# A state-space layer and a mixture of experts: read-backs turned ahead of weight splits in the routed tiles, and the choice of experts in five parts

## The reference

```
attention half:  x = layer_norm(feat);  x = x @ in_proj.T (1024 -> 96);  conv of 3 taps, silu
                 selective scan over the rows (96 channels, 16 states);  out = y @ out_proj.T + feat
feed-forward:    scores = sigmoid(x @ router_w)                      # 32 experts in 8 groups of 4
                 4 groups by the sum of their two best scores; in them the 8 best experts of a row
                 weights = their scores, made to sum to 2.5
                 routed = sum over the 8 of weight * (silu(x @ gate_e) * (x @ up_e)) @ down_e
                 shared = silu(x @ sw_gate) * (x @ sw_up) @ sw_down
                 out = routed + shared + the attention half
```

## Time and profile before

| | |
|---|---|
| timed runs | 11768.19 us median of 3 (11751.63 to 11770.12) |
| profiled execution | 11704.35 us, span 11702.8 us |
| busy: TensorE | 11303.2 us, 97% |
| VectorE, ScalarE, GpSimd | 4611.8, 2989.1, 4299.9 us |
| mean granted TensorE clock | 0.985 |
| DMA | 1451.51 MB, mean 124 GB/s |

### The profile page before, as it was taken

The page is one execution under the profiler, slowest core; times in us unless marked ns, Lnnn a source line. Parts: engine busy times, 40 slices in busy tenths (PEclk is TensorE's granted clock), DMA queues, the critical chain, the costliest instruction groups (busy, mean ns, idle before and its releaser), DMA issues.

```text
span 11702.8 us, 200733 instructions
## 1 busy us (share of the span) xinstructions
PE 11303.2 (97%) x50496; PEld 9279.1 (79%) x50497; DVE 4611.8 (39%) x6239; ACT 2989.1 (26%) x4098; POOL 4299.9 (37%) x4236
## 2 busy tenths in 40 slices
PE   8999689998999999999999999999998999999998
PEld 7888467776888888888888888878887787888887
DVE  5666566664232323333323233232334323223222
ACT  2122244442222222222222222222223223222221
POOL 2555442222333333333333333333333333333333
PEclk9999799999999999999999999999999999999999
DMA  4333366675444444454544454454555545444443
GB/s 160 132 132 133 110 168 178 179 177 148 96 115 100 117 96 118 119 136 99 137 97 119 97 156 98 97 134 96 137 143 158 140 97 155 97 97 117 97 97 85
DMA packets 918208, 1451.51 MB, mean 124 GB/s; under 512 B 314530, under 2 KB 585058, under 8 KB 895048
## 3 DMA queue, kind: packets, MB, share of 16 engines
q0 software_dynamic: 212800, 623.06, 25.2%
q10 hardware_dynamic: 384512, 383.85, 11.8%
q1 hardware_dynamic: 320776, 443.28, 11.5%
HBM read 853.67 MB, written 596.15 MB: 124 GB/s over the span
## 4 chain that ended last, share of the span: by engine, by line
PE 64%; DVE 3%; issue 3%; DMA 3%; ACT 1%; DVEq 1%; ACTq 1%; POOL 0%; SPq 0%; POOLq 0%
PE pd L2002 22%; PE pg L66 7%; PE pg L67 7%; PE pu L66 7%; PE pg L68 7%; PE pu L68 7%; PE pu L67 7%; DMA activated<-av 2%; DVE w_lo L1908 2%; ACT w_hi L1817 1%; DMA aq<-activated 1%; ACTq L1589 1%; DVEq L1589 0%; DVE aT L1931 0%; DVE xT L1920 0%
## 5 line engine op out<-in xcount | busy, mean ns | idle before, releaser
L1772 POOL DMA_INDIRECT xq<-xn_rows,idx_q x2124 | 2191.5, 1032 | 936.6 <-issue 485.2
L1780 POOL DMA_INDIRECT out_rows<-y,idx_s x528 | 865.9, 1640 | 4472.0 <-issue 4462.2
L1956 DVE SCALAR_TENSOR_TENSOR av<-pu,scale,sg 128x512 f32<-128x512 f32 x528 | 396.6, 751 | 3598.3 <-PE pu L68 3537.3
L66 PE MATMUL pg<-w_hi,x_hi 128*128 128x512 f32 x4224 | 1645.5, 390 | 49.5 <-DVE x_lo L1924 39.4
L66 PE MATMUL pu<-w_hi,x_hi 128*128 128x512 f32 x4224 | 1644.2, 389 | 6.0 <-DVEq L1973 6.0
L67 PE MATMUL pg<-w_lo,x_hi 128*128 128x512 f32 x4224 | 1644.5, 389 | 0.0
L68 PE MATMUL pg<-w_hi,x_lo 128*128 128x512 f32 x4224 | 1644.4, 389 | 0.0
L67 PE MATMUL pu<-w_lo,x_hi 128*128 128x512 f32 x4224 | 1643.2, 389 | 0.0
L68 PE MATMUL pu<-w_hi,x_lo 128*128 128x512 f32 x4224 | 1643.2, 389 | 0.0
L1821 ACT ACTIVATE x_hi<-xT 128x1024 fp32r<-128x1024 f32 x530 | 562.8, 1062 | 3885.4 <-DVE xT L1920 3885.4
L2002 PE MATMUL pd<-w_hi,a_hi 128*128 128x512 f32 x4224 | 1143.6, 393 | 91.7 <-ACT a_hi L1837 91.3
(11 more groups left out here) (286 smaller groups left out, 14560.9 us busy)
## 6 DMA issues: line engine op xcount, KB each, us to landing
stage<-in_w_all SPq DMA_DIRECT2D x174, 1024.0 KB, 8.6
activated<-av ACTq DMA_DIRECT2D x528, 256.0 KB
aq<-activated ACTq DMA_DIRECT2D x528, 256.0 KB
rep<-steps ACTq DMA_DIRECT2D x192, 512.0 KB
xq<-xn_rows,idx_q POOLq DMA_INDIRECT x2124
xt<-in_x SPq DMA_DIRECT2D x64, 512.0 KB, 4.6
xn_rows<-xn SPq DMA_DIRECT2D x64, 512.0 KB, 2.6
xn_turned<-sx_hi SPq DMA_DIRECT2D x64, 512.0 KB
```

The source lines that it names most:

```text
L66: m(dst, hi, whi[:, cols], start=begin, stop=False)
L1772: g.indirect_dma_start(out=xq[q][:, n], out_offset=None, in_=xn_q, in_offset=bass.IndirectOffsetOnAxis(ap=idx_q[q][:, n:n + 1], axis=0))\
L1780: g.indirect_dma_start(out=out, out_offset=bass.IndirectOffsetOnAxis(ap=idx_s[q][:, 0:1], axis=0), in_=y[q][:], in_offset=None, compute_op ...
L1956: v.scalar_tensor_tensor(out=av[:], in0=pu[:], scalar=scale[q][:].bitcast(F32), in1=sg[:], op0=ALU.mult, op1=ALU.mult).then_inc(av_ready, 1)
```

## The change

In the routed tiles: VectorE turns the read-back activations ahead of the low halves of new down weights; ScalarE issues the read-back right behind the store, ahead of `x_high`; SP asks for the gate and up weights of t+2 ahead of the down weights of t+1; `fresh` and `runs` are loaded once, ahead of the condition and (ScalarE) of the wait for the gate product. In routing: `route` has five parts, run at k=1 (0 and 1), k=2, k=3 and k=0 of the chunk behind, and the turning of z and its copy and store move one step with them.

```diff
@@ SP, routing: the store of z goes behind the turned rows and the output of its step
-                    if k == 3 and not known(c, 0):
-                        store_z(c - 1, 1 - r)
                     if not ends(c, k, 1):
                         store_turned(*later(c, k, 1))
                     if not (known(c, 0) and k == 0):
                         store_out(*later(c, k, -1))
+                    if k == 3 and not known(c, 0):
+                        store_z(c - 1, 1 - r)
@@ ScalarE, routing
-                    if k == 2 and not known(c, 0):
+                    if k == 3 and not known(c, 0):
                         z_row(c - 1, 1 - r)
@@ TensorE, routing
-                    if k == 1 and not known(c, 0):
+                    if k == 2 and not known(c, 0):
                         z_turned(c - 1)
@@ VectorE, routing: part 1 is cut behind max_index
                     for j in range(J):
                         last = v.max_index(i8[:, j], v8[:, j], masked[:, j])
                     s(last)
+                if part == 2:
                     s(v.tensor_copy(i8f[:], i8[:]))
...
                     if k == 0 and not (known(c, 0) or known(c, 1)):
-                        route(c - 2, r, 3)
-                    if k < 3 and not known(c, 0):
-                        route(c - 1, 1 - r, k)
+                        route(c - 2, r, 4)
+                    if k and not known(c, 0):
+                        for part in ((0, 1), (2,), (3,))[k - 1]:
+                            route(c - 1, 1 - r, part)
@@ SP, experts
+                with sp.If(value_of(sp, fresh, t + 2, 1) > 0):
+                    load(t + 2, (0, 1, 2, 3))
+                with sp.Else():
+                    sp.sem_inc(sp_passed, 1)
                 with sp.If(value_of(sp, fresh, t + 1, 1) > 0):
                     load(t + 1, (4, 5))
-                with sp.Else():
-                    sp.sem_inc(sp_passed, 1)
-                with sp.If(value_of(sp, fresh, t + 2, 1) > 0):
-                    load(t + 2, (0, 1, 2, 3))
@@ ScalarE, experts
-                    with act.If(value_of(act, fresh, t - 1, 1) > 0):
-                        down_high(t - 1)
+                    new = value_of(act, fresh, t - 1, 1)
+                    run = value_of(act, runs, t - 1, E)
+                    with act.If(new > 0):
+                        down_high(t - 1, run)
...
+                new = value_of(act, fresh, t + 1, 1)
+                run = value_of(act, runs, t + 1, E)
                 act.wait_ge(gate_done, t + 1)
...
                 store_activated(t)
+                load_activated(t)
                 x_high(t + 2, q)
                 if begun:
-                    evict(t - 1, 1 - q, 0)
-                load_activated(t)
-                if begun:
-                    evict(t - 1, 1 - q, 1)
+                    for h in range(2):
+                        evict(t - 1, 1 - q, h)
@@ VectorE, experts
-                    with dve.If(value_of(dve, fresh, t - 1, 1) > 0):
-                        lows(t - 1, (4, 5))
+                    new = value_of(dve, fresh, t - 1, 1)
+                    run = value_of(dve, runs, t - 1, E)
+                    turn_activated(t - 1)
+                    with dve.If(new > 0):
+                        lows(run, (4, 5))
                     with dve.Else():
                         dve.sem_inc(dve_passed, 1)
                 dve.sem_inc(down_weights, 1)
-                turn_activated(t - 1)
                 a_low(t - 1)
...
-                with dve.If(value_of(dve, fresh, t + 1, 1) > 0):
-                    lows(t + 1, (0, 1))
+                new = value_of(dve, fresh, t + 1, 1)
+                run = value_of(dve, runs, t + 1, E)
+                with dve.If(new > 0):
+                    lows(run, (0, 1))
...
                 activated(t, q, half)
-                with dve.If(value_of(dve, fresh, t + 1, 1) > 0):
-                    lows(t + 1, (2, 3))
+                with dve.If(new > 0):
+                    lows(run, (2, 3))
```

More of the change, by code:

```diff
@@ L683, in route @@
             def route(c, i, part):
-                s = Steps(dve, rt_step, c * RT + (0, 7, 17, 21)[part], dve_passed)
+                s = Steps(dve, rt_step, c * RT + (0, 7, 14, 17, 21)[part], dve_passed)
                 if part == 0:
@@ L731, in route @@
                     s(last)
+                    assert s.n == 7, s.n
+                if part == 2:
                     s(v.tensor_copy(i8f[:], i8[:]))
@@ L741, in route @@
                     s(last)
-                    assert s.n == 10, s.n
-                if part == 2:
+                    assert s.n == 3, s.n
+                if part == 3:
                     s(v.tensor_reduce(w8[:].rearrange("p j k -> p (j k)"), prod[:], AX.X, ALU.add))
@@ L753, in route @@
                     assert s.n == 4, s.n
-                if part == 3:
+                if part == 4:
                     dve.wait_ge(rank_ready, c + 1)
@@ L795, in _ @@
             a_low(NT - 1)
-            route(NC - 2, 0, 3)
+            route(NC - 2, 0, 4)
             route(NC - 1, 1, 0)
             summed(NC - 1, J - 1)
-            route(NC - 1, 1, 1)
-            route(NC - 1, 1, 2)
-            route(NC - 1, 1, 3)
+            for part in range(1, 5):
+                route(NC - 1, 1, part)
 def scan_stage(nc, T, B, io):
@@ L1844, in evict, with down_high @@
                 a.activation(y[q][:, h * 512:(h + 1) * 512], pd[h][:], ACT.Copy).then_inc(y_ready, 1)
-            def down_high(t):
-                run = 0 if isinstance(t, int) else value_of(act, runs, t, E)
+            def down_high(t, run):
                 wait_past(act, down_done, t * 2)
@@ L1855, in begin @@
                 if isinstance(t, int):
-                    down_high(t - 1)
+                    down_high(t - 1, 0)
                 else:
-                    with act.If(value_of(act, fresh, t - 1, 1) > 0):
-                        down_high(t - 1)
+                    new = value_of(act, fresh, t - 1, 1)
+                    run = value_of(act, runs, t - 1, E)
+                    with act.If(new > 0):
+                        down_high(t - 1, run)
                     with act.Else():
@@ L1870, in tile @@
                 a.activation(sg[:], pg[:], ACT.Silu).then_inc(sg_ready, 1)
-                with act.If(value_of(act, fresh, t + 1, 1) > 0):
-                    run = value_of(act, runs, t + 1, E)
+                with act.If(new > 0):
                     for k in (0, 1):
@@ L1909, in low, with lows @@
                     .then_inc(split_lo[q // 2], 1)
-            def lows(t, qs, known=None):
-                run = value_of(dve, runs, t, E) if known is None else known
+            def lows(run, qs):
                 for k in qs:
@@ L1940, in begin @@
                 if isinstance(t, int):
-                    lows(t - 1, (4, 5), 0)
-                else:
-                    with dve.If(value_of(dve, fresh, t - 1, 1) > 0):
-                        lows(t - 1, (4, 5))
+                    turn_activated(t - 1)
+                    lows(0, (4, 5))
+                else:
+                    new = value_of(dve, fresh, t - 1, 1)
+                    run = value_of(dve, runs, t - 1, E)
+                    turn_activated(t - 1)
+                    with dve.If(new > 0):
+                        lows(run, (4, 5))
                     with dve.Else():
@@ L1981, in _ @@
             turn_rows(0, 0, 0)
-            lows(0, (0, 1), 0)
+            lows(0, (0, 1))
             dve.sem_inc(gate_weights, 1)
             x_low(0, 0)
-            lows(0, (2, 3), 0)
+            lows(0, (2, 3))
             dve.sem_inc(up_weights, 1)
```

## The result

The changed kernel takes 11731.4 us (median of 12 runs, 11722.4 to 11741.0), the kernel before, timed beside it, 11769.2 (12 runs, 11751.6 to 11779.5): ratio 0.9967, interval 0.9960 to 0.9974. That is 38 us faster where 106 had been forecast; 11731 lies above the range of 11622 to 11720. The profiled execution took 11727.17 us (span 11725.6), longer than the 11704.35 of the profile before. So two questions stand: where most of the gain went, and why the two profiles say the opposite of the timed runs.

The account below looks back on a forecast made before the run. TensorE's matmul streaming was taken as the bound, with only waits at expert changes and in routing to win. Routed stage -80.6 and routing -25.7 gave -106.3 us: 11598 by the profile, 11662 us timed, range 11622 to 11720.

Parts of the forecast that it names:

- Part 3: Routed tiles, ScalarE: read-back issued ahead of x_high; from below 0 to above 0.7 us a change, taken as 0.
- Part 1: Tile f+1, second after an expert change: turning before low halves ends its wait; 1 us, behind one-tile experts 4.3 us.
- Part 2: Tile f, first of a new expert: values loaded once and earlier on VectorE and ScalarE, net 0.8 us earlier.
- Part 4: SP's gate and up loads first: 2.5 us for each of 4 one-tile f; pair in a row 12.7 with Part 1.
- Rival A: Routed tiles: down loads hold the read-back, one-tile f term turns from -10 to +14.4; 11691 us, chance 0.14.
- Part 5: Routing, choice in five parts: all VectorE blocks below 9.6 us, so 23 TensorE waits go; -25.7 us net.
- The main forecast: Whole kernel: all terms hold, routed stage -80.6 and routing -25.7 us; 11662 us, chance 0.56.
- Rival C: Routing keeps a wait through the GpSimd hold, block 10.3 us, 0.7 us in 12 chunks; 11670 us, chance 0.12.
- Carrying the 0.5% over: Whole kernel: timed median lies 0.5% above the profiled execution; the difference was carried over, 11598 to 11662 us.
- Rival B: Routed tiles: the wait only changes its name, to VectorE's low halves; about -55 us, 11713 us, chance 0.10.

Follow-up runs that it names:

- e4: The kernel before with only the routed tiles' edits, routing as before: 11754.0 us, -16.7 us, ratio 0.9986.
- e13: The changed kernel, unchanged, timed again as a reference: 11742.2 us, 0.9957 of the kernel before.
- e14: The changed kernel with x_high ahead of the read-back again, run beside e13: 11694.3 us, 0.9916 of the kernel before.
- e8: The changed kernel with x_high ahead of the read-back and down weights asked for first again, and value loads moved to idle time: 11658.5 us.
- e1: The kernel before, unchanged, profiled once more: 11773.3 us, profiled execution 11770.4 us.
- e5: The changed kernel with SP asking for the down weights first again: 11710.1 us, 1.0002 of the kernel before.
- e11: The changed kernel with x_high ahead of the read-back, value loads in idle time and SP's load order chosen by need: 11730.4 us.
- e18: The kernel before with the routed tiles' edits, but x_high still ahead of the read-back: 11648.2 us against 11700.9, ratio 0.9954.
- e6: The same kernel as e14, on a chip of the faster kind: 11650.6 us, 0.9952 of the kernel before.
- e15: The kernel before with turning the activations ahead of the low halves as its only edit: 11748.9 us, -41.2 us, ratio 0.9965.

## Why the prediction was wrong

The direction was right, the size wrong by 68 us, and one step carries 48 of them. About 16 more are missing in the routed tiles: -16.7 in e4 and the 47.9 of part 3 would make -64.6 for -80.6, which is an estimate across two groups.

- **Part 3, "I take 0", between "below 0" and 0.7 us a change: the step that failed.** I asked what the read-back's landing gains and found nothing, rightly. I did not ask what the moved wait holds up: ScalarE, x_hi and both evictions behind it, then x_lo, the turn, a_hi, sg and the high halves. Measured +47.9 us (e13, e14), in ordinary f (17.80 against 16.36), 4-apart changes (18.97 against 16.32) and f of one-tile experts (25.50 against 23.27).
- **Part 1** was right, and more: f+1 17.31 to 16.35 us (forecast -1), one-tile f+1 27.46 to 23.44 (-4.0, forecast -4.3); alone -41 us.
- **Part 2**: VectorE's 0.78 us between av and the low halves went. ScalarE's 0.49 only moved: "the loads stand ahead of the wait for the gate", but that wait was over, and now two loads stand between a_hi and sg, 0.67 us at tile 144. "Net for tile f: 0.8 us earlier" failed by this and part 3; with the loads in idle time 9.6 us came back (e8).
- **Part 4**: the pair 372, 373 gained 13.1 us in the result's trace and 11.9 from e1 to e14, forecast 12.7; the 104.39 us stretch took 93.32 and not "about 88", as its f got longer. The one-tile f's (-2.5 each) got 0.0 without part 3 (e14 23.27, e1 23.32), and the 58.27 us stretch nothing (58.32, forecast -5). Rival A's mechanism is there: at tile 290 VectorE turns 16.0 us into the tile, 2.6 later than before, in this row of the trace after (the tile starts at 7690.87):

```profile
7706.88 0.71 DVE L1933 STREAM_TRANSPOSE aT<-aq 128x512 f32<-128x512 f32 x1 [4.75 <-DMA aq<-activated]
```

 The order accounts for part of that (f of one-tile experts is 24.56 in e5 without it, 25.50 in e13). That the down loads can hold the read-back is what e5 and e11 show.
- **Part 5**: -25.7 forecast, -23.7 measured, and that agreement is luck. "All are below 9.6, so the 23 waits go" failed: the waits at k=1 went, those at k=2 rose from 1.3 to up to 2.0 us. The main forecast left the GpSimd hold with prod; it lies where the add runs, on z, 2.8 us, so the block is 10.7 and not 7.9. Rival C had named just that, at 10.3 us and a wait of 0.7. And z's turning, which left k=1, took 0.7 us of TensorE time ahead of that deadline with it; this was not tested by itself. On kind A, which the rows were read from, chunks 3 to 14 go from 974.1 to 969.6 us (e18, e6), a sixth of the 26.0. The gain on kind B comes from gaps that those rows don't have: 1011.9 us (e1) to 984.6 (the result's trace), or 1031.7 (e15) to 991.5 (e14).
- **Carrying the 0.5% over** came out right as a level and wrong as a reading: the difference goes with the chip, and all but 5 us of it lie ahead of the routed tiles, not spread over them.
- Without part 3 the same steps give -95.8 us on kind B (e14), near the -106.3 of the sum, but -56.8 on kind A (e6), for which the sum was made. Rival B's 11713 us came nearest, for another reason: its new wait for VectorE is there, but 9.6 us long. Part 3 had no rival of its own.

## What to carry to other kernels

A wait moved forward in an in-order engine is charged with everything behind it: follow the instructions that it passes to their own readers before calling the move free. Moving the turn ahead of the weight splits was worth 41 us, as what it waited for was there already; moving the read-back ahead of x_hi cost 48, as what it waits for was not. An order of DMAs has to be looked at across queues: two loads that slip in front of a read-back hold it though they stand on another engine's queue. And profile on the chip that is timed, or know how its stalls differ.

## What the runs showed of the hardware

- The same kernel took 11701 to 11707 us on two chips and 11770 to 11790 on a third. A good half of the difference between the two profiles is in chunks 3 to 14 of routing, 974.0 and 1011.9 us, with gaps of 1 to 3 us in front of VectorE's short instructions that no other engine explains. The routed stage differs by 5 us.
- Such gaps can come in long runs. In chunk 15 of the changed kernel TensorE stands 1.5 to 1.7 us ahead of about every second matmul, over some 18 us, and its granted clock is 0.76 over that tile (the lower level, 1.2 GHz, in part of it). No transfer of instructions starts between 1305 and 1343 us, where the 16 KB ones before came every 21 to 29 us; that fits a wait for code, and doesn't prove it:

```profile
1330.38 0.37 PE L525 MATMUL lg<-wcat,xnT 128*128 128x128 f32 x1 [1.52 <-issue]
...
1333.18 0.37 PE L525 MATMUL lg<-wcat,xnT 128*128 128x128 f32 x1 [1.72 <-issue]
```

- Two stalls of one engine can cover each other: taking GpSimd's 2.8 us hold away brought up 2.4 us of waits that no other engine ended, on the chip of kind B only.
- A 256 KB store issued 8 to 10 us behind four loads of 1 MB landed 17.3 to 17.4 us after their issue, in both kernels. A 256 KB read-back took 6.7 us to its turn with the first of two 1 MB loads issued 0.35 us ahead of it on the other queue (e11), and 2.6 us with it 1.4 us behind (e8).
